# Expert products from two fp16 parts with power-of-two scales, and another order of loads, in an attention and mixture-of-experts kernel

## The chip, the cores and the metric

One core of one Trainium2 chip runs the whole program. The metric is the device time of one launch in microseconds (us), here the median of three runs. The profile is of one execution; its span runs from the first to the last instruction.

## The reference, cut to what matters

The input is x (16 batches of 100 tokens, 256 features). A cross-attention (16 heads, 361 context rows) adds to x. Then a soft mixture of experts adds again:

```python
x = x + xattn(layernorm(x), ctx, ctx, mask, ...)
z = layernorm(layernorm(x), norm_g, norm_b)
se = layernorm(slot_embeds, slot_g, slot_b) * scale
logits = einsum('bnd,esd->bnes', z, se)                  # 16 experts, 64 slots each
dispatch = softmax(logits, axis=tokens)
combine = softmax(logits over all 1024 slots)
slots = einsum('bnd,bnes->besd', z, dispatch)
gate = gelu(slots @ Wg[e] + bg[e])                       # 256 -> 512
up = slots @ Wu[e] + bu[e]
eout = (gate * up) @ Wd[e] + bd[e]                       # 512 -> 256
out = x + einsum('bns,bso->bno', combine, eout)
```

All inputs are fp32, and so is the output. The last row reads the x after attention.

## The kernel before, in words

The program has three blocks one after the other, with a barrier between them: `attention_phase`, `routing_phase` and `expert_phase`. Every engine has its own list of instructions, written out by hand; semaphores tie the lists together.

**Attention** treats the 16 batches in a pipeline. Its last steps also make the normalised tokens of batch 0 for routing (lines 577 to 599).

**Routing** treats one batch in each step t. PE makes the logits (L1167), ACT copies them to `l_sb` (L1075), DVE takes the maxima (L1002, L1024), ACT makes the exponentials (L1084, L1103), PE transposes, DVE and ACT copy to `dispT` and `combT`, and SP stores both to DRAM. DVE also makes the normalised tokens of a later batch (L1027 to L1048), which ACT keeps in `xn`. Between these steps the first two experts are made ready: `load_gate_up` (POOL), `weights_hi` (ACT) and `weights_lo` (DVE); and the last two steps make the first slots (`first_slots`, L1224, L1232, L1240).

**Experts.** The 16 experts come in 8 pairs: pair 0, a loop over pairs 1 to 6, pair 7. Each pair is treated for two halves h of the batches (8 batches, 512 rows of slots), each half for its two experts e, so there are 32 units u of work. In a unit, PE makes for each of four blocks c of 128 hidden features the `gate` and the `up` product (L1539). A product in fp32 is replaced by three products of two parts, a high and a low one:

```python
for wt, st in ((wgu_h, slot_h), (wgu_h, slot_l), (wgu_l, slot_h)):
    for kc in range(2):
        mm = nc.tensor.matmul(bank[:], wt[e][...], st[h][...], start=(k == 0), stop=(k == 5))
```

The high part is a copy rounded to float32r, the low part is the value minus the high one, also float32r. After the product of block c, ACT makes the gelu (`gate_sb`, L1486), DVE adds the bias of up and multiplies (L1430), ACT rounds to `hid_h` (L1490), DVE subtracts to `hid_l` (L1435). Behind block c PE also makes a piece of the slots of the next half (c = 0 and 2, L1512) or of the output of the last one (c = 1 and 3, L1519), both in plain fp32, with the pieces `slot_h` and `slot_l` (L1473, L1406) and the addition to x (L1415) behind them. Then come the 48 `down` products of the unit (L1579): in `DOWN_ORDER` the first 18 need `hid_h` and `hid_l` of blocks 0 to 2 only, the 19th needs block 3. DVE adds the bias `bd` and writes `eo` in two parts g (L1453); part 0 can start behind the 36th product. SP moves `eo` to `eo_pair`.

The weights of the next pair are split once per pair: `wgu_h` (L1274, ACT) and `wgu_l` (L1279, DVE) behind units (h=1, e=0) and (h=1, e=1), for expert 0 and 1; `wd_h` (L1496) and `wd_l` (L1441) inside the units of h=0, at c=1 and c=2. POOL issues the loads of weights, of `disp` and of `comb`, and waits for each buffer to come free.

## Time and profile before

| | us |
|---|---|
| median of 3 runs (1162.72 to 1166.11) | 1164.14 |
| the profiled execution | 1163.88 |
| its span | 1162.2 |
| PE busy | 1063.1 |
| DVE busy | 698.5 |
| ACT busy | 576.3 |
| POOL busy | 332.6 |

In the timeline attention ends at 356 us, routing at 501 us, and the experts take the rest. "Busy" of PE counts each matmul from its start to its modelled end; matmuls overlap, so their pace is read from start to start. The granted clock is given as a share of full speed: 1.00 is 2.4 GHz and 0.50 is 1.2 GHz.

### The profile page before, as it was taken

The numbers are of one execution on the slowest core, as the hardware profiler recorded it, in microseconds if no ns is written. First come the engines' busy times: TensorE is split into PE (matmuls) and PEld (weight loads), VectorE is DVE, ScalarE is ACT, GpSimd is POOL, SyncE is SP. The second block draws the span as 40 slices with busy tenths as digits, with TensorE's granted clock in tenths as the row PEclk, the third lists the DMA queues.
The fourth block names the chain that finished last, engine by engine and source line by source line (L and its number), as shares of the span: only waits on it lengthen the run. The fifth ranks groups of instructions, "written<-read, shape, count | busy, mean of one in ns | idle before, by whom it ended". The sixth has DMA issues, their size and how long they took to land.

```text
span 1162.2 us, 22171 instructions
## 1 busy us (share of the span) xinstructions
PE 1063.1 (91%) x7172; PEld 869.9 (75%) x7172; DVE 698.5 (60%) x1247; ACT 576.3 (50%) x1084; POOL 332.6 (29%) x348
## 2 busy tenths in 40 slices
PE   5688999999877888789999999999999999999997
PEld 3466777777663444478888888888888888888885
DVE  5556777777636888544555555655645555556544
ACT  2376878778655788733433343433424334333421
POOL 5267767667664343210010010100100100100000
PEclk8789999999958999889999999999999999999998
DMA  8858778678403534432142242432331331422123
GB/s 208 183 120 142 168 156 159 155 140 172 88 2 96 145 99 112 122 129 65 41 132 75 56 117 74 107 103 76 113 92 41 113 93 41 131 74 54 47 57 83
DMA packets 115080, 121.50 MB, mean 105 GB/s; under 512 B 46633, under 2 KB 105445, under 8 KB 115029
## 3 DMA queue, kind: packets, MB, share of 16 engines
q1 hardware_dynamic: 100908, 79.07, 30.5%
q0 software_dynamic: 10960, 40.67, 11.5%
q10 hardware_dynamic: 3160, 1.11, 0.6%
q8 instruction: 28, 0.46, 0.2%
q14 instruction: 24, 0.19, 0.1%
HBM read 73.87 MB, written 29.93 MB: 89 GB/s over the span
## 4 chain that ended last, share of the span: by engine, by line
PE 55%; DVE 1%; issue 1%; ACT 0%; DVEq 0%; ACTq 0%
PE down L1579 16%; PE gate L1539 15%; PE up L1539 15%; PE mix L1519 5%; PE mix L1512 4%; DVE gate_sb L1430 0%; ACT hid_h L1490 0%; DVE hid_l L1435 0%; DVE wd_l L1441 0%; DVE x L1415 0%; ACT gate_sb L1486 0%; DVE slot_l L1406 0%; DVEq L1633 0%; DVEq L1429 0%; DVEq L1412 0%
## 5 line engine op out<-in xcount | busy, mean ns | idle before, releaser
L1486 ACT ACTIVATE gate_sb<-gate,bgu 128x512 f32<-128x512 f32 x128 | 88.1, 689 | 222.3 <-PE gate L1539 207.7
L402 POOL TENSOR_TENSOR p_l<-p_f,p_h 121x800 f16<-121x800 f32 (+1 forms) x96 | 163.7, 1718 | 80.4 <-ACT p_h L652 79.5
L1490 ACT ACTIVATE hid_h<-gate_sb 128x512 fp32r<-128x512 f32 x128 | 80.9, 632 | 178.0 <-DVE gate_sb L1430 178.0
L1430 DVE SCALAR_TENSOR_TENSOR gate_sb<-up,bgu,gate_sb 128x512 f32<-128x512 f32 x128 | 95.9, 749 | 103.1 <-PE up L1539 101.3
L486 DVE TENSOR_REDUCE head_max<-at_rows 100x2 f32<-100x722 f32 x124 | 112.9, 910 | 71.8 <-PE at_rows L730 69.8
L1579 PE MATMUL down<-wd_h,hid_h 128*128 128x256 f32 x512 | 150.7, 294 | 0.7 <-DVE hid_l L1435 0.7
L1435 DVE TENSOR_TENSOR hid_l<-gate_sb,hid_h 128x512 fp32r<-128x512 f32 x128 | 88.6, 692 | 93.6 <-ACT hid_h L1490 93.6
L1579 PE MATMUL down<-wd_l,hid_h 128*128 128x256 f32 x512 | 144.8, 283 | 0.0
L1579 PE MATMUL down<-wd_h,hid_l 128*128 128x256 f32 x512 | 144.8, 283 | 0.0
L1263 POOL DMA_DIRECT2D wd<-in_Wd x16 | 12.2, 766 | 320.8 <-DVE eo L1453 300.4
L1579 PEld LDWEIGHTS down<-wd_h,hid_h 128*128 128x128 f32 x512 | 98.0, 191 | 3.4 <-issue 1.0
L1453 DVE TENSOR_TENSOR eo<-down,bd 128x512 f32<-128x512 f32 x64 | 44.3, 692 | 93.3 <-PE down L1579 93.3
L1579 PEld LDWEIGHTS down<-wd_l,hid_h 128*128 128x128 f32 x512 | 98.2, 192 | 0.8
L1579 PEld LDWEIGHTS down<-wd_h,hid_l 128*128 128x128 f32 x512 | 98.1, 192 | 0.0
L647 ACT ACTIVATE p_f<-at_cols 121x800 f32<-121x800 f32 (+1 forms) x96 | 79.7, 830 | 30.4 <-PE at_cols L742 29.4
L1539 PE MATMUL gate<-slot_h,wgu_h 128*128 128x512 f32 x256 | 91.0, 436 | 4.0 <-PEq L1631 4.0
L730 PE MATMUL at_rows<-kt,qt 100*100 100x362 f32 x248 | 74.5, 383 | 12.2 <-DVE head_max L486 11.4
L652 ACT ACTIVATE p_h<-p_f 121x800 f16<-121x800 f32 (+1 forms) x96 | 83.6, 871 | 3.0
L1539 PE MATMUL gate<-slot_l,wgu_h 128*128 128x512 f32 x256 | 80.7, 397 | 0.0
L1539 PE MATMUL up<-slot_l,wgu_h 128*128 128x512 f32 x256 | 80.1, 394 | 0.0
L742 PE MATMUL at_cols<-qt,kt 104*121 104x200 f32 (+1 forms) x384 | 67.8, 303 | 13.4 <-DMA qt<-max_p 8.8
L1539 PE MATMUL up<-slot_h,wgu_h 128*128 128x512 f32 x256 | 80.0, 394 | 0.0
(165 smaller groups left out, 2279.1 us busy)
## 6 DMA issues: line engine op xcount, KB each, us to landing
eo_pair<-eo SPq DMA_DIRECT2D x128, 128.0 KB, 2.4
k_parts<-kq_n SPq DMA_DIRECT2D x16, 724.0 KB, 3.7
kt<-k_parts SPq DMA_DIRECT2D x32, 362.0 KB
wgu<-in_Wg POOLq DMA_DIRECT2D x16, 512.0 KB, 6.2
wgu<-in_Wu POOLq DMA_DIRECT2D x16, 512.0 KB, 6.9
wd<-in_Wd POOLq DMA_DIRECT2D x16, 512.0 KB, 5.2
combine<-combT SPq DMA_DIRECT2D x16, 400.0 KB, 4.0
dispatch<-dispT SPq DMA_DIRECT2D x16, 400.0 KB
```

What stands on the lines that cost most here:

```text
L402: nc.gpsimd.tensor_tensor(p_l[i][0:kn, :, 0:N], p_f[i][0:kn], p_h[i][0:kn, :, 0:N], ALU.subtract).then_inc(p_low, 1)
L486: nc.vector.tensor_reduce(head_max[:, :, r], bank[0:N, :, 0:S], AX.X, ALU.max).then_inc(max_ready, 1)
L647: nc.scalar.activation(p_f[u][0:kn].rearrange("k (g e) n -> k g (e n)", g=2), cols_ps[0:kn, :, 0:4 * N], ACT.Exp, scale=1.0 / SCALE_INV).t ...
L652: nc.scalar.activation(p_h[u][0:kn, :, 0:N], p_f[u][0:kn], ACT.Copy).then_inc(p_hi, 1)
L730: mm = nc.tensor.matmul(bank[0:N, c, 0:SW], q[0:ROWS_A, r, N * c:N * c + N], k[0:ROWS_A, r, :], start=True, stop=True)
L742: mm = nc.tensor.matmul(cols_ps[0:kn, e // 2, (e % 2) * 2 * N:(e % 2 + 1) * 2 * N], kt[t % NBUF][0:ROWS_B, r, j * KC:j * KC + kn], qt[t % ...
L1430: nc.vector.scalar_tensor_tensor(gate[c % 2][:], up_ps[c % 2][:], bu_col(bgu, pair, e, c), gate[c % 2][:], ALU.add, ALU.mult).then_inc(hid ...
L1435: nc.vector.tensor_tensor(hid_l[:, c, :], gate[c % 2][:], hid_h[:, c, :].bitcast(F32), ALU.subtract).then_inc(hidl_ready, 1)
L1486: nc.scalar.activation(gate[c % 2][:], gate_ps[c % 2][:], ACT.Gelu, bias=bg_col(bgu, pair, e, c)).then_inc(gelu_ready, 1)
L1490: nc.scalar.activation(hid_h[:, c, :], gate[c % 2][:], ACT.Copy).then_inc(hidh_ready, 1)
L1539: mm = nc.tensor.matmul(bank[:], wt[e][:, kc, i, c * P:(c + 1) * P], st[h][:, kc, e, :, :].rearrange("p b s -> p (b s)"), start=(k == 0), ...
L1579: mm = nc.tensor.matmul(down_ps[t // 2][:, t % 2, :], ht[:, c, t * P:(t + 1) * P], wt[:, c, :], start=(c == 0 and k == 0), stop=(c == FC - ...
```

## The change

**Types.** `wgu_h`, `wgu_l`, `wd_h`, `wd_l`, `slot_h`, `slot_l`, `hid_h` and `hid_l` become float16 in place of float32r. The list of matmuls on PE is the same, instruction by instruction. Accumulation stays in fp32.

**Scales.** A float16 has little range, so every operand is multiplied by a power of two. For the slots the scale comes from a bound, the largest magnitudes of `norm_g` and `norm_b` (new `norm_scaled` on DVE at the end of attention; both vectors are multiplied once, and the logits are divided again in the copy to `l_sb`). For the weights it comes from the largest magnitude of each expert's weights: new reductions on DVE (`max_gate_up`, `max_down`, `max_hidden_bias`), which give a maximum per partition; SP stores them to DRAM and reads all of them back to every partition (`share_maxima`); then `expert_scales` on DVE makes a chain of 14 small operations, with a wait between those that depend on each other. Copies to high parts get a `scale` operand on ACT, and the subtractions to low parts on DVE become SCALAR_TENSOR_TENSOR (multiply, subtract), as does the addition of `bd`. ACT gets a marker instruction (`sem_inc(waited)`) ahead of `hid_h` and `wd_h`.

**Order.** The maxima of the next pair are taken in unit (h=0, e=1) for gate and up and in (h=1, e=0) for down, the scales in (h=1, e=1) at c=2. Both `wgu_h` and both `wgu_l` now come behind unit (h=1, e=1). The loads of `Wd` and of half of `disp` come earlier in POOL's list, the load of `bd` apart from that of `Wd`. In routing `wgu_h` of expert 0 moves from t=1 to t=15, ahead of the copy to `l_sb`; `wgu_l` of expert 0 too moves to t=15; the maxima stand at t=1, 2 and 12, the scales at t=14.

**Semaphores.** Several are merged into one; nothing else in attention moves.

The core of the diff:

```diff
-        "wgu_h": [sb(f"wgu_h{e}", [P, 2, 2, F], F32R) for e in range(2)],
-        "wgu_l": [sb(f"wgu_l{e}", [P, 2, 2, F], F32R) for e in range(2)],
+        "wgu_h": [sb(f"wgu_h{e}", [P, 2, 2, F], F16) for e in range(2)],
+        "wgu_l": [sb(f"wgu_l{e}", [P, 2, 2, F], F16) for e in range(2)],
         "wd": [sb(f"wd{e}", [P, FC, D], F32) for e in range(2)],
...
         def step(b, t):
             for s in range(SLOTS_RT):
                 part(s + SLOTS_RT, b - 1, t - 1)
                 part(s, b, t)
-            if t == 1:
+            if t in (1, 2):
+                max_gate_up(nc, dve, keep, t - 1, 0)
+            if t == B - 4:
+                for e in range(2):
+                    max_down(nc, dve, keep, e, 0)
+                dve.wait_ge(keep["bias_in"], 32)
+                max_hidden_bias(nc, dve, keep, 0)
+            if t == B - 2:
+                expert_scales(nc, dve, keep, 0)
+            if t == B - 1:
                 weights_lo(nc, dve, keep, 0, 0)
             if t in (B - 1, B):
...
+def share_maxima(eng, keep, pair):
+
+    eng.wait_ge(keep["max_ready"], MAXIMA * pair + MAXIMA)
+    eng.sem_inc(keep["waited"], 1)
+    if not (isinstance(pair, int) and pair == 0):
+        eng.wait_ge(keep["scale_step"], SCALE_STEPS * pair)
+    eng.sem_inc(keep["waited"], 1)
+    flat = keep["max_dram"]
+    eng.dma_start(flat.rearrange("(p j) -> p j", p=P), keep["maxima"][:].rearrange("p k e -> p (k e)")).then_inc(keep["max_moved"], 16)
+    eng.wait_ge(keep["max_moved"], 32 * pair + 16)
+    eng.sem_inc(keep["waited"], 1)
+    eng.dma_start(keep["all_maxima"][:], flat.partition_broadcast(P)).then_inc(keep["max_moved"], 16)
+
...
+def expert_scales(nc, dve, keep, pair):
...
+    def done(n):
+        dve.wait_ge(step, SCALE_STEPS * pair + n)
+        dve.sem_inc(keep["waited"], 1)
+
+    dve.wait_ge(keep["max_moved"], 32 * pair + 32)
+    if not (isinstance(pair, int) and pair == 0):
+        done(0)
+    nc.vector.tensor_reduce(top[:, 0:3, :].rearrange("p k e -> p (k e)"), keep["all_maxima"][:].rearrange("q (p j) -> q j p", p=P), AX.X, ALU.max).then_inc(step, 1)
+    done(1)
...
 def weights_hi(nc, act, keep, e, pair):
     act.wait_ge(keep["wgu_in"][e], 32 * pair + 32)
-    nc.scalar.activation(keep["wgu_h"][e][:], keep["wgu"][e][:], ACT.Copy).then_inc(keep["wh_ready"][e], 1)
+    act.wait_ge(keep["scale_step"], SCALE_STEPS * pair + SCALE_STEPS)
+    act.sem_inc(keep["waited"], 1)
+    nc.scalar.activation(keep["wgu_h"][e][:], keep["wgu"][e][:], ACT.Copy, scale=keep["w_scale"][:, bass.ds(pair, 1), 0, e]).then_inc(keep["wh_ready"][e], 1)
 
 
 def weights_lo(nc, dve, keep, e, pair):
     dve.wait_ge(keep["wh_ready"][e], pair + 1)
-    nc.vector.tensor_tensor(keep["wgu_l"][e][:], keep["wgu"][e][:], keep["wgu_h"][e][:].bitcast(F32), ALU.subtract).then_inc(keep["wl_ready"][e], 1)
+    dve.sem_inc(keep["waited"], 1)
+    nc.vector.scalar_tensor_tensor(keep["wgu_l"][e][:], keep["wgu"][e][:], keep["w_scale"][:, bass.ds(pair, 1), 0, e], keep["wgu_h"][e][:],
+                                   ALU.mult, ALU.subtract).then_inc(keep["wl_ready"][e], 1)
 
...
                         for odd in range(2):
                             sp.dma_start(dst[:, 2 * g:2 * g + 2, odd, :], eo[e][odd * SL:(odd + 1) * SL, 2 * g:2 * g + 2]).then_inc(eo_moved[h][e][g], 16)
+                    if h == 1 and e == 0 and not last:
+                        share_maxima(sp, keep, pair + 1)
...
-                pool.wait_ge(slots_done, 4 * (2 * pair + 2))
+                pool.wait_ge(wdl_ready[0], pair + 1)
                 pool.sem_inc(waited, 1)
-                for h in range(2):
-                    hb = slice(BH * h, BH * h + BH)
-                    pool.dma_start(disp[:, hb], at(dispatch_dram, pair + 1)[:, hb]).then_inc(disp_in[h], 16)
+                load_down(pool, a, keep, 0, pair + 1)
+                load_slot_weights(pair + 1, 0, 4 * (2 * pair + 1))
             if not first:
                 pool.wait_ge(comb_done, 8 * pair)
                 pool.sem_inc(waited, 1)
                 pool.dma_start(comb[:], at(combine_dram, pair)).then_inc(comb_in, 16)
             if not last:
+                pool.wait_ge(wdl_ready[1], pair + 1)
+                pool.sem_inc(waited, 1)
+                load_down(pool, a, keep, 1, pair + 1)
+                load_slot_weights(pair + 1, 1, 4 * (2 * pair + 2))
                 for e in range(2):
                     pool.wait_ge(eo_ready, 2 * (4 * pair + 2 + e) + 2)
                     pool.sem_inc(waited, 1)
-                    load_down(pool, a, keep, e, pair + 1)
+                    load_down_bias(pool, a, keep, e, pair + 1)
...
                         if not (first and h == 0 and e == 0):
                             dve.wait_ge(down_done, 2 * u)
-                        nc.vector.tensor_tensor(hid_l[:, c, :], gate[c % 2][:], hid_h[:, c, :].bitcast(F32), ALU.subtract).then_inc(hidl_ready, 1)
+                        nc.vector.scalar_tensor_tensor(hid_l[:, c, :], gate[c % 2][:], keep["hid_scale"][:, bass.ds(2 * pair + e, 1)], hid_h[:, c, :],
+                                                       ALU.mult, ALU.subtract).then_inc(hidl_ready, 1)
                         if h == 0 and c == 2:
 
                             dve.wait_ge(wdh_ready[e], pair + 1)
                             if not first:
                                 dve.wait_ge(down_done, 2 * u - 2)
-                            nc.vector.tensor_tensor(wd_l[e][:], wd[e][:], wd_h[e][:].bitcast(F32), ALU.subtract).then_inc(wdl_ready[e], 1)
+                            nc.vector.scalar_tensor_tensor(wd_l[e][:], wd[e][:], keep["w_scale"][:, bass.ds(pair, 1), 1, e], wd_h[e][:],
+                                                           ALU.mult, ALU.subtract).then_inc(wdl_ready[e], 1)
                         r = 2 * e + c // 2
                         if c % 2 == 0 and nxt:
                             dve.wait_ge(slots_done, 4 * (hs + 1) + r + 1)
                             slots_lo(hs + 1, 1 - h, r)
                         if c % 2 == 1 and prev:
                             combine_add(hs - 1, 1 - h, r, first)
+                        if h == 1 and e == 1 and c == 2 and not last:
+                            expert_scales(nc, dve, keep, pair + 1)
                     for g in range(2):
+                        if h == 0 and e == 1 and not last:
+                            max_gate_up(nc, dve, keep, g, pair + 1)
+                        if h == 1 and e == 0 and not last:
+                            max_down(nc, dve, keep, g, pair + 1)
+                            if g == 1:
+                                max_hidden_bias(nc, dve, keep, pair + 1)
                         dve.wait_ge(down_done, 2 * u + g + 1)
                         if not (first and h == 0):
                             dve.wait_ge(eo_moved[1 - h][e][g], 32 * pair + 32 * h)
-                        dve.wait_ge(wd_in[e], 32 * pair + 32)
-                        nc.vector.tensor_tensor(eo[e][:, 2 * g:2 * g + 2, :], down_ps[g][:],
-                                                bd[e][:].rearrange("p (o d) -> p o d", o=1).broadcast_to([P, 2, D]), ALU.add).then_inc(eo_ready, 1)
-                    if h == 1 and not last:
-                        weights_lo(nc, dve, keep, e, pair + 1)
+                        dve.wait_ge(keep["bd_in"][e], 16 * pair + 16)
+                        dve.sem_inc(waited, 1)
+                        nc.vector.scalar_tensor_tensor(eo[e][:, 2 * g:2 * g + 2, :], down_ps[g][:], keep["un_down"][:, bass.ds(2 * pair + e, 1)],
+                                                       bd[e][:].rearrange("p (o d) -> p o d", o=1).broadcast_to([P, 2, D]),
+                                                       ALU.mult, ALU.add).then_inc(eo_ready, 1)
+                        if h == 1 and e == 1 and not last:
+                            weights_lo(nc, dve, keep, g, pair + 1)
             if last:
                 for r in range(4):
                     combine_add(2 * pair + 1, 1, r, False)
...
-                        weights_hi(nc, act, keep, e, pair + 1)
+                    if h == 1 and e == 1 and not last:
+                        for x in range(2):
+                            act.wait_ge(up_done, FC * (u - 1 + x) + FC)
+                            weights_hi(nc, act, keep, x, pair + 1)
 
         pairs(act, step)
```

**The order of instructions** is shown at two places. The first is DVE in the loop over the pairs, unit (h=1, e=1), from c=3 to the jump back. Before (`gate_sb` is the product of gate and up, `eo` the expert's output, `wgu_l` the low part of the next pair's weights):

```order
L1430 SCALAR_TENSOR_TENSOR gate_sb<-up,bgu,gate_sb 128x512
L1435 TENSOR_TENSOR hid_l<-gate_sb,hid_h 128x512
L1410 REGISTER_ALU
L1415 SCALAR_TENSOR_TENSOR x<-mix,rz,x 100x256 x2
L1449 REGISTER_ALU
L1453 TENSOR_TENSOR eo<-down,bd 128x512
L1449 REGISTER_ALU
L1453 TENSOR_TENSOR eo<-down,bd 128x512
L1279 TENSOR_TENSOR wgu_l<-wgu,wgu_h 128x2048
L1331 REGISTER_ALU
L1331 COMPARE_AND_BRANCH
```

Now, in the changed kernel:

```order
L1581 SCALAR_TENSOR_TENSOR gate_sb<-up,bu_s,gate_sb 128x512
L1586 SCALAR_TENSOR_TENSOR hid_l<-gate_sb,hid_scale,hid_h 128x512
L1561 REGISTER_ALU
L1566 SCALAR_TENSOR_TENSOR x<-mix,rz,x 100x256 x2
L1610 REGISTER_ALU
L1615 SCALAR_TENSOR_TENSOR eo<-down,un_down,bd 128x512
L1415 REGISTER_ALU
L1417 SCALAR_TENSOR_TENSOR wgu_l<-wgu,w_scale,wgu_h 128x2048
L1610 REGISTER_ALU
L1615 SCALAR_TENSOR_TENSOR eo<-down,un_down,bd 128x512
L1417 SCALAR_TENSOR_TENSOR wgu_l<-wgu,w_scale,wgu_h 128x2048
L1470 REGISTER_ALU
```

`wgu_l` of expert 0 has come in between the two `eo`. Ahead of this piece, behind `slot_l` of c=2, stand the 14 operations on `top`, `w_scale`, `un_gate`, `bu_s`, `hid_scale` and `un_down`, which were not there before.

The second place is ACT in routing at t=15. Before, the piece was:

```order
L1084 ACTIVATE e_comb,z_tok<-l_sb,neg_max 100x1024
L1103 ACTIVATE e_disp,z_slot<-rt_lT,neg_max_s 128x100 x8
L1075 ACTIVATE l_sb<-rt_logits 100x1024
L1274 ACTIVATE wgu_h<-wgu 128x2048
L1091 ACTIVATE combT<-rt_out 128x400 x2
L1232 ACTIVATE slot_h<-rt_slots 128x4x2x64
L1232 ACTIVATE slot_h<-rt_logits 128x4x2x64
```

and now:

```order
L1147 ACTIVATE e_disp,z_slot<-rt_lT,neg_max_s 128x100 x8
L1411 ACTIVATE wgu_h<-wgu,w_scale 128x2048
L1118 ACTIVATE l_sb<-rt_logits,norm_top 100x1024
L1411 ACTIVATE wgu_h<-wgu,w_scale 128x2048
L1135 ACTIVATE combT<-rt_out 128x400 x2
L1281 ACTIVATE slot_h<-rt_slots 128x4x2x64
L1281 ACTIVATE slot_h<-rt_logits 128x4x2x64
```

The copy to `l_sb` of the last batch stands behind `wgu_h` of expert 0, and that one waits for the scales.

## Rows read from the trace of the kernel before

**Rows 1.** The page, part 1: busy time of each engine, share, instructions.
```profile
PE 1063.1 (91%) x7172; PEld 869.9 (75%) x7172; DVE 698.5 (60%) x1247; ACT 576.3 (50%) x1084; POOL 332.6 (29%) x348
```

**Rows 2.** Windows of 40 us: PE, PEld, DVE, ACT, POOL busy (instructions), clock, DMA share, GB/s.
```profile
840.00:880.00 40.00, 40.00 (x239) 35.19 (x238) 21.42 (x34) 13.13 (x21) 1.68 (x3) 1.00 0.26 72
880.00:920.00 40.00, 40.00 (x239) 35.25 (x238) 23.98 (x34) 16.28 (x23) 5.44 (x8) 1.00 0.36 95
```

**Rows 3.** The page, part 5: ACT's first parts, busy, mean ns, idle before.
```profile
L1490 ACT ACTIVATE hid_h<-gate_sb 128x512 fp32r<-128x512 f32 x128 | 80.9, 632 | 178.0 <-DVE gate_sb L1430 178.0
```

**Rows 4.** Timeline of PE in a pair: start, length in us, engine, line, instruction.
```profile
807.62 0.62 PE L1539 MATMUL gate<-slot_l,wgu_h 128*128 128x512 f32 x2
...
809.44 0.62 PE L1539 MATMUL up<-slot_h,wgu_l 128*128 128x512 f32 x2
...
821.53 0.47 PE L1579 MATMUL down<-wd_h,hid_h 128*128 128x256 f32 x1
821.84 0.28 PE L1579 MATMUL down<-wd_l,hid_h 128*128 128x256 f32 x1
...
827.35 0.28 PE L1579 MATMUL down<-wd_h,hid_l 128*128 128x256 f32 x1
```

**Rows 5.** Timeline of PE in attention: first and last of 15 16-bit matmuls in a row.
```profile
204.49 0.18 PE L762 MATMUL at_out<-v,p_l 121*128 121x49 bf16 x1
...
204.84 0.18 PE L762 MATMUL at_out<-v,p_l 121*128 121x49 bf16 x1
```

**Rows 6.** Timeline of DVE in routing: small operations one behind the other.
```profile
418.91 1.22 DVE L1002 TENSOR_REDUCE neg_max<-l_sb 100x1 f32<-100x1024 f32 x1
420.05 0.15 DVE L1007 RECIPROCAL rz<-z_tok 100x1 f32 x1
420.12 0.56 DVE L1024 TENSOR_REDUCE neg_max_s<-rt_lT 128x4 f32<-128x400 f32 x1
...
422.03 0.18 DVE L1038 BATCH_NORM_AGGREGATE rt_mv<-rt_st 100x2 f32<-100x6 f32 x1 [0.15 <-DVE rt_st L1035]
```

**Rows 7.** Timeline of DVE, h=1, e=1, from c=2 to the first eo.
```profile
817.40 0.75 DVE L1430 SCALAR_TENSOR_TENSOR gate_sb<-up,bgu,gate_sb 128x512 f32<-128x512 f32 x1 [0.71 <-PE up L1539]
...
819.46 0.68 DVE L1406 TENSOR_TENSOR slot_l<-mix,slot_h 128x512 fp32r<-128x512 f32 x1
821.05 0.75 DVE L1430 SCALAR_TENSOR_TENSOR gate_sb<-up,bgu,gate_sb 128x512 f32<-128x512 f32 x1 [0.92 <-PE up L1539]
822.50 0.69 DVE L1435 TENSOR_TENSOR hid_l<-gate_sb,hid_h 128x512 fp32r<-128x512 f32 x1 [0.70 <-ACT hid_h L1490]
...
826.23 0.69 DVE L1453 TENSOR_TENSOR eo<-down,bd 128x512 f32<-128x512 f32 x1 [2.25 <-PE down L1579]
```

**Rows 8.** Timeline of DVE: end of attention; routing at t=1 and t=14.
```profile
338.58 0.56 DVE L518 TENSOR_REDUCE o_sum<-at_out 100x128 f32<-100x384 f32 x1 [5.15 <-PE at_out L762]
...
377.02 2.29 DVE L1279 TENSOR_TENSOR wgu_l<-wgu,wgu_h 128x2048 fp32r<-128x2048 f32 x1 [0.46 <-ACT wgu_h L1274]
...
481.61 1.29 DVE L1018 COPY dispT<-rt_out 100x512 f32<-100x512 f32 x2 [3.31 <-PE rt_out L1152]
```

**Rows 9.** Timeline of ACT: the last batch of routing.
```profile
481.37 1.07 ACT L1075 ACTIVATE l_sb<-rt_logits 100x1024 f32<-100x1024 f32 x1
482.27 1.97 ACT L1274 ACTIVATE wgu_h<-wgu 128x2048 fp32r<-128x2048 f32 x1
```

**Rows 10.** Timeline of DVE, h=0, e=0: gate of c=2 and hid_l of c=3.
```profile
837.84 0.75 DVE L1430 SCALAR_TENSOR_TENSOR gate_sb<-up,bgu,gate_sb 128x512 f32<-128x512 f32 x1 [0.71 <-PE up L1539]
...
843.08 0.69 DVE L1435 TENSOR_TENSOR hid_l<-gate_sb,hid_h 128x512 fp32r<-128x512 f32 x1 [0.70 <-ACT hid_h L1490]
```

**Rows 11.** Timeline of PE: start of the down products of that half.
```profile
841.86 0.47 PE L1579 MATMUL down<-wd_h,hid_h 128*128 128x256 f32 x1
```

**Rows 12.** Timeline of PE in routing: the same products at the two clocks.
```profile
468.21 6.12 PE L1167 MATMUL rt_logits<-seT,rt_xnT 128*100 128x512 f32 x8 [2.94 <-ACT rt_xnT L1112]
...
477.46 3.68 PE L1167 MATMUL rt_logits<-seT,rt_xnT 128*100 128x512 f32 x8
```

206 lines of the change are left out of this document (149 added, 57 removed).

## Prediction

> **What bounds the kernel now.** I read the views in this order. The page's busy times show PE in front, 1063.1 of 1162.2 us, with DVE at 698.5 [rows 1]. That is a mean over three blocks, so the windows come next: in the expert block PE is busy for 40.00 of every 40 us at a clock of 1.00 (2.4 GHz), while DVE has 21.4 and 24.0 and ACT 13 and 16 [rows 2]. Two thirds of the time are thus PE's own pace, and the wait of ACT's `hid_h` for DVE, 178.0 us in sum, costs nothing [rows 3]. The timeline gives that pace. Eight gate and up products lie between 807.62 and 809.44: 0.2275 us each for 512 columns. The down products start every (827.35 − 821.84)/46 = 0.1198 us for 256 columns [rows 4]. At 2.4 GHz the columns alone would take 0.2133 and 0.1067, so a float32r product pays a surcharge of 14.2 and 13.1 ns. Last I read how late DVE delivers what PE needs, because the change gives DVE more work at three places.
>
> I count in the time of the profiled execution, 1163.88 us (span 1162.2, so 1.7 lie around it); the median is 0.3 above it. About 0.3% can be told from no change, 3.5 us.
>
> **PE's products.** Their list stays. The nearest row for a 16-bit pair of weight load and product is attention's: 14 steps from 204.49 to 204.84, 25.0 ns for 49 columns, of which 20.4 are columns; surcharge 4.6 ns [rows 5]. So short a product may be held by something else, so I take 3.5 ns; the bounds are 0 (bare columns) and 14 (no gain). Gate and up gain 10.7 ns, down 9.6. A unit has 48 of each: 0.51 + 0.46 = 0.97 us; 32 units: **−31** (bounds −42 and 0). The Trainium skill, TensorE: Matmul & The Clock Gate, section Back-to-back issue gap, gives columns over 2.4 plus 2.5 ns for a warm product; by it the gain would be −34.
>
> **Scales at the end of each pair (7 times).** `expert_scales` stands on DVE behind `slot_l` of c=2 in unit (h=1, e=1), ahead of the multiplication of c=3, behind which `hid_h`, `hid_l` and PE's 19th down product are queued. No row shows this chain; I build it. A reduction of 1024 took 1.22 and one of 400 took 0.56, which makes 0.93 for its 768 elements. A small operation takes 0.15, an independent one starts 0.07 behind the last, and a dependent one 0.15 behind the end of its source [rows 6]. Eight waits: 0.93 + 8×0.15 + the operations, 7×0.15 + 6×0.08 = 3.7 us. The bounds: all back to back, 0.93 + 13×0.07 = 1.8; twice the handover, since in the loop each wait needs register work, 5.
>
> Where it bites, counted from the multiplication of c=2 at 817.40 [rows 7]: `slot_l` ends 2.74 later. The marker on ACT and the change of `hid_l` from TENSOR_TENSOR (0.69) to SCALAR_TENSOR_TENSOR (0.75) add 0.06 + about 0.1 (estimate: the difference between a handover with a marker, 0.15 [rows 6], and one without, half of 0.70 − 0.63 [rows 3, 7]). The chain starts at 2.9 and ends at 6.6. From the multiplication of c=3 to the end of `hid_l` it is 822.50 + 0.69 − 821.05 = 2.14, with 0.16 added 2.3: 8.9, and PE hears it at 9.0. PE wants it for its 19th product: 821.84 + 17×0.12 − 817.40 = 6.5 before, and 0.3 less with quicker products: 6.2. **Stall 2.8 us.**
>
> The data for the chain are there: the maxima end with unit (1,0), two DMAs of 2 to 3 us follow, and the chain stands some 17 us behind. The maxima themselves (two of 2.3 us in (0,1), two of 1.2 in (1,0)) lie beside PE's down products: DVE is idle for 2.25 us ahead of the first `eo` [rows 7], and they end before the next unit's first multiplication, so I cost them at nothing. With that cover gone they would cost up to 2 us a pair. All the added work, some 12 us a pair, raises DVE from 23 to 29 of 40 us: not a bound.
>
> **`wgu_l` of expert 0 (7 times).** Before, it lay behind unit (1,0), with a whole unit to spare. Now it lies between the two `eo` of (1,1), and PE's next instruction is a gate product that waits for it. The first `eo` starts at 826.23; the down products end at 827.35 + 0.12 = 827.47, 1.24 later [rows 4, 7], with quicker products 1.12. DVE needs 0.75 for `eo` (SCALAR_TENSOR_TENSOR now) and 2.29 + 0.06 for `wgu_l` [rows 8]: ready 2.0 behind the end, with the handover **2.1 us** of stall. The bounds are 1.8 and 2.4. ACT has both `wgu_h` done by then (2×1.97 [rows 9] from the end of `hid_h` of c=3). `wgu_l` of expert 1 ends about when the first multiplication of the new pair is due. Both stalls: 4.9 × 7 = **+34** (bounds 7×2.7 = 19 and 7×6.4 = 45).
>
> **Units of h=0.** From the multiplication of c=2 (837.84) to the end of `hid_l` of c=3 (843.77) it is 5.93 [rows 10]; here `wd_l` stands in between and DVE is full, so every addition counts: two markers and three changes to SCALAR_TENSOR_TENSOR, 0.4. With the handover 6.5. PE wants it at 841.86 + 0.31 + 17×0.12 − 837.84 = 6.4 [rows 4, 11], now 6.1. Stall 0.4, 15 units: **+6** (0 to 8). In units of h=1 0.2 us are left over, so no stall.
>
> **Routing.** At t=1 a reduction of 2048 takes the place of `wgu_l` (2.29 [rows 8]), and ACT loses a copy; the one at t=2 is new on the busiest engine: together +1.5 (0 to 2.5). At t=12 the added 2.6 us meet the stretch in which the logits ran at half the clock (6.12 us against 3.68 [rows 12]) and all waited for them: +0.2. At t=14 the scales start when `dispT` ends (482.8 [rows 8]), 3.7, handover 0.2, `wgu_h` 1.9, and only then `l_sb`, which started at 481.37 [rows 9]: it starts at 488.6, 7.2 late, and everything to the block's end hangs on it. `wgu_l` at t=15 delays the last `rz_slot` by 1 more. Sum **+10** (5 to 13).
>
> **Attention.** `norm_scaled` (3 us) falls into DVE's idle 5.15 us ahead of 338.58 [rows 8]: 0. The moved loads of `Wd` and `disp` only come earlier, and `comb` now goes ahead of half of `disp`: 0. SP waits in `share_maxima` while it has nothing else: 0.
>
> **Sum:** 1163.9 − 31 + 34 + 6 + 10 = 1183 us. The gain is real, but the price of getting the scales is larger.
>
> **Rivals.**
> 1. *VectorE gets quicker too.* If its operations with 16-bit operands ran at twice the pace, `wgu_l` would take 1.3 in place of 2.3, and `hid_l` and `slot_l` 0.3 less each. Second stall −1.0, first −0.9, h=0 gone, routing −1.5: 1183 − 7×1.9 − 6 − 1.5 = 1162; with the chain at its lower bound (−1.9 at 8 places) **1147**. It ends on the faster side once the low parts save 1 us at a boundary and the chain is under 3.3. For it: types are halved. Against: one operand of each is still fp32. Chance 0.08.
> 2. *The 16-bit product beats its columns.* The same section of the skill also gives about 131 ns per product for a stream of 512-column pairs. As a mechanism of this kernel: PE would fall behind DVE, which has 29 of 40 us of work and waits for ACT in each block; a unit would take some 16 us in place of 20.3, and the time about 1040. The 25 ns for 49 columns [rows 5] speak against it. Chance 0.02.
> 3. *The clock falls at the boundaries.* PE stands still for 2.8 and 2.1 us with 3.3 us of work between. In routing, an idle 2.94 us ended in logits at half the clock (1.2 GHz) [rows 12]. Each boundary would then run a few us at half pace and lose about 2.5: 1183 + 18 = **1201**. Against it: the engine is full before and behind. Chance 0.15.
> 4. *The change doesn't do what it says:* the surcharge belongs to any load of 128 columns. Then 1183 + 31 = **1214**. The 16-bit rows of attention [rows 5] speak against it. Chance 0.04.
> 5. *The chain is short,* 2 us or less, as its operations overlap, and the surcharge is gone entirely: 1183 − 8×1.8 − 11 = **1158**. For it: the 0.07 between independent operations. Against: eight links are dependent. Chance 0.1.
>
> My forecast, 1170 to 1195 with its own bounds, has 0.61. The range of 8 in 10 goes from 1157 to 1201: it leaves out rivals 2 and 4 and half of 1. Faster by over 0.3%: rivals 1 (0.07), 2 and 5 (0.06): 0.15. Within 0.3%: the rest of rival 5 and the low end of mine, 0.06. Slower: 0.79.
>
> **What would show it.** Gate spacing 0.217 and down spacing 0.110; PE idle ahead of the 19th down product of (1,1) by 2.8 us, released by `hid_l`; idle ahead of the first gate product of a pair by 2.1, released by `wgu_l`; idle of 0.4 in the down products of h=0; the expert block starting near 511 in place of 501.4. I am wrong if the spacing stays at 0.228 and 0.120, if PE shows no idle time at the boundary, or if the chain on `top` takes under 2 us or over 5.

## The result, and the profile after

| | before | after |
|---|---|---|
| median, us | 1164.39 (4 runs) | 1215.23 (4 runs, 1212.36 to 1217.61) |
| the profiled execution, us | 1163.88 | 1217.13 |
| its span, us | 1162.2 | 1215.5 |

The ratio of after to before is 1.0435, with a 95% interval of 1.0404 to 1.0467: 51 us slower. The forecast had the sign (slower, chance 0.79) and the places, but said 19 us slower with a range up to 1201. The time lies outside it.

The page of the changed kernel, part 1, and windows of its expert block (columns as in [rows 1, 2]):

```profile
PE 1058.3 (87%) x7172; PEld 707.6 (58%) x7172; DVE 794.4 (65%) x1409; ACT 602.4 (50%) x1084; POOL 333.3 (27%) x349
...
800.00:840.00 40.00, 39.63 (x246) 25.46 (x245) 28.32 (x39) 14.83 (x21) 1.89 (x3) 1.00 0.24 70
840.00:880.00 40.00, 33.58 (x178) 19.80 (x176) 24.34 (x42) 17.14 (x21) 3.96 (x6) 0.91 0.32 95
```

PE is no longer busy for 40 of 40 us. A window without the end of a pair still has 39.6 at full clock; one with it has 33.6, and the granted clock is under 1. So most of the loss in the expert block sits at the ends of pairs. PE's timeline at one of them (unit (h=1, e=1) and the first products of the next pair) shows what:

```profile
767.18 0.27 PE L1747 MATMUL down<-wd_h,hid_l 128*128 128x256 f16 x1
...
768.49 0.27 PE L1747 MATMUL down<-wd_h,hid_l 128*128 128x256 f16 x1
773.13 0.27 PE L1747 MATMUL down<-wd_h,hid_h 128*128 128x256 f16 x1 [4.37 <-DVE hid_l L1586]
...
774.49 0.42 PE L1747 MATMUL down<-wd_h,hid_l 128*128 128x256 f16 x1
774.70 0.42 PE L1747 MATMUL down<-wd_h,hid_h 128*128 128x256 f16 x1
...
777.96 0.27 PE L1747 MATMUL down<-wd_h,hid_l 128*128 128x256 f16 x1
779.66 0.59 PE L1707 MATMUL gate<-slot_h,wgu_h 128*128 128x512 f16 x2 [1.43 <-DVE wgu_l L1417]
...
782.24 1.06 PE L1680 MATMUL mix<-disp,xn 100*128 100x128 f32 x8
```

The spacings first: 12 down products from 767.18 to 768.49, 0.1092 us each (0.1198 before, [rows 4]); 12 gate and up products from 779.66 to 782.24, 0.215 us (0.2275 before). Then an idle time of 4.37 us ahead of the 19th down product, released by `hid_l`. Then a stretch in which the same products start 0.21 apart; the granted clock is 0.50 there (1.2 GHz). Between 774.1 and 777.6 some sixteen products lose 0.1 us each, 1.7 us. Then an idle time of 1.43 us for `wgu_l`. At the next pair end that one was 2.05, and the slow stretch came in two pieces, the second behind the stall for `wgu_l`:

```profile
866.22 0.96 PE L1707 MATMUL gate<-slot_h,wgu_h 128*128 128x512 f16 x2 [2.05 <-DVE wgu_l L1417]
866.97 1.06 PE L1707 MATMUL gate<-slot_l,wgu_h 128*128 128x512 f16 x2
...
870.06 0.59 PE L1707 MATMUL up<-slot_h,wgu_l 128*128 128x512 f16 x2
```

DVE's timeline ahead of the 773.13 of PE, from the multiplication of c=2 to `hid_l` of c=3:

```profile
762.39 0.75 DVE L1581 SCALAR_TENSOR_TENSOR gate_sb<-up,bu_s,gate_sb 128x512 f32<-128x512 f32 x1 [0.26 <-PE up L1707]
...
765.31 1.51 DVE L1378 TENSOR_REDUCE top<-all_maxima 128x6 f32<-128x768 f32 x1
766.99 0.17 DVE L1381 TENSOR_SCALAR top<-top 128x4 f32<-128x4 f32 x1 [0.16 <-DVE top L1378]
...
768.78 0.59 DVE L1393 TENSOR_SCALAR bu_s<-bgu,w_scale,norm_top  x2 [0.28 <-DVE top L1390]
...
770.38 0.16 DVE L1404 SCALAR_TENSOR_TENSOR un_down<-top 128x2 f32 x1
770.58 0.75 DVE L1581 SCALAR_TENSOR_TENSOR gate_sb<-up,bu_s,gate_sb 128x512 f32<-128x512 f32 x1
772.23 0.75 DVE L1586 SCALAR_TENSOR_TENSOR hid_l<-gate_sb,hid_scale,hid_h 128x512 f16<-128x512 f32 x1 [0.90 <-ACT hid_h L1655]
```

The chain starts 2.92 us behind the multiplication (forecast 2.9) and takes 5.3 to the next one, 765.31 to 770.58 (forecast 3.7, upper bound 5).

From the starts of the units in PE's timeline, a table of the six pairs of the loop (four units each, start to start, us):

| kernel | (0,0) | (0,1) | (1,0) | (1,1) | mean pair |
|---|---|---|---|---|---|
| before | 20.32 | 20.32 | 20.32 | 20.32 | 81.3 |
| after | 19.86 to 21.56 | 19.85 | 19.2 to 19.4 | 27.0 to 27.8 | 87.0 |

At least two of four units, and mostly three, are faster than before. The fourth gives back more than all four gain. The first unit has 21.56 where a slow stretch runs into it. The granted clock falls to 0.50 behind the stalls at all seven pair ends.

Routing: the expert block's first gate product starts at 516.60 (501.37 before). ACT's timeline of the last batch, which answers to [rows 9], and the `dispT` of that batch on DVE:

```profile
485.69 0.26 ACT L1147 ACTIVATION_READ_ACCUMULATOR e_disp<-rt_lT,neg_max_s 128x1 f32 x1
492.20 2.00 ACT L1411 ACTIVATE wgu_h<-wgu,w_scale 128x2048 f16<-128x2048 f32 x1 [6.25 <-DVE un_down L1404]
494.11 1.10 ACT L1118 ACTIVATE l_sb<-rt_logits,norm_top 100x1024 f32<-100x1024 f32 x1
...
486.02 1.29 DVE L1050 COPY dispT<-rt_out 100x512 f32<-100x512 f32 x2 [3.31 <-PE rt_out L1194]
```

`l_sb` starts 8.1 us behind the `dispT` of that batch (486.02); before, it started 0.2 ahead of it (481.37 and 481.61, [rows 8, 9]).

The start of the expert block also holds what attention took in that one execution: the first `l_sb` of routing came at 363.43 here, at 362.50 before, and between 361 and 369 in the profiles of the experiments, which leave attention as it is. So routing is best counted from its first `l_sb` to the first gate product: 138.9 us before, 153.2 after, 14.3 more.

### The profile page after: what moved, and what is told of

The parts are those of the page before. It is cut to its first block, busy times and chain, and to the rows that moved or that the text cites. A ratio compares the mean times of both kernels' runs of the same rounds, so it can differ in the third digit from the quotient of the medians.

```text
span 1215.5 us, 22832 instructions
## 1 busy us (share of the span) xinstructions
PE 1058.3 (87%) x7172; PEld 707.6 (58%) x7172; DVE 794.4 (65%) x1409; ACT 602.4 (50%) x1084; POOL 333.3 (27%) x349
## 3 DMA queue, kind: packets, MB, share of 16 engines
q10 hardware_dynamic: 3160, 1.11, 0.5%
## 4 chain that ended last, share of the span: by engine, by line
PE 43%; DVE 7%; issue 4%; ACT 2%; DMA 0%; DVEq 0%; ACTq 0%
PE gate L1707 13%; PE up L1707 12%; PE down L1747 11%; PE mix L1680 4%; PE mix L1687 3%; DVE gate_sb L1581 2%; ACT hid_h L1655 2%; DVE hid_l L1586 2%; DVE wgu_l L1417 1%; DVE top L1378 1%; DMA disp<-dispatch 0%; ACT slot_h L1636 0%; DVE slot_l L1557 0%; DVE wd_l L1593 0%; ACT wd_h L1663 0%
## 5 line engine op out<-in xcount | busy, mean ns | idle before, releaser
L1649 ACT ACTIVATE gate_sb<-gate,bgu,un_gate 128x512 f32<-128x512 f32 x128 | 99.2, 775 | 207.6 <-PE gate L1707 201.5
L1655 ACT ACTIVATE hid_h<-gate_sb,hid_scale 128x512 f16<-128x512 f32 x128 | 92.4, 722 | 207.2 <-DVE gate_sb L1581 207.2
L1747 PE MATMUL down<-wd_h,hid_h 128*128 128x256 f16 x512 | 146.0, 285 | 38.9 <-DVE hid_l L1586 36.8
L1586 DVE SCALAR_TENSOR_TENSOR hid_l<-gate_sb,hid_scale,hid_h 128x512 f16<-128x512 f32 x128 | 96.2, 752 | 121.5 <-ACT hid_h L1655 121.5
L1747 PE MATMUL down<-wd_l,hid_h 128*128 128x256 f16 x512 | 146.0, 285 | 0.0
L1747 PE MATMUL down<-wd_h,hid_l 128*128 128x256 f16 x512 | 146.0, 285 | 0.0
L1581 DVE SCALAR_TENSOR_TENSOR gate_sb<-up,bu_s,gate_sb 128x512 f32<-128x512 f32 x128 | 96.0, 750 | 59.8 <-PE up L1707 52.4
L1707 PE MATMUL gate<-slot_h,wgu_h 128*128 128x512 f16 x256 | 77.3, 384 | 15.6 <-DVE wgu_l L1417 10.4
L1707 PE MATMUL up<-slot_h,wgu_h 128*128 128x512 f16 x256 | 77.5, 385 | 0.0
L1707 PE MATMUL gate<-slot_h,wgu_l 128*128 128x512 f16 x256 | 77.5, 385 | 0.0
L1707 PE MATMUL gate<-slot_l,wgu_h 128*128 128x512 f16 x256 | 77.4, 384 | 0.0
```

The lines of the kernel that those rows point to most:

```text
L1581: nc.vector.scalar_tensor_tensor(gate[c % 2][:], up_ps[c % 2][:], keep["bu_s"][:, bass.ds(2 * pair + e, 1), c], gate[c % 2][:], ALU.add, A ...
L1586: nc.vector.scalar_tensor_tensor(hid_l[:, c, :], gate[c % 2][:], keep["hid_scale"][:, bass.ds(2 * pair + e, 1)], hid_h[:, c, :], ALU.mult, ...
L1649: nc.scalar.activation(gate[c % 2][:], gate_ps[c % 2][:], ACT.Gelu, bias=bg_col(bgu, pair, e, c), scale=keep["un_gate"][:, bass.ds(2 * pai ...
L1655: nc.scalar.activation(hid_h[:, c, :], gate[c % 2][:], ACT.Copy, scale=keep["hid_scale"][:, bass.ds(2 * pair + e, 1)]).then_inc(hidh_ready, 1)
L1707: mm = nc.tensor.matmul(bank[:], wt[e][:, kc, i, c * P:(c + 1) * P], st[h][:, kc, e, :, :].rearrange("p b s -> p (b s)"), start=(k == 0), ...
L1747: mm = nc.tensor.matmul(down_ps[t // 2][:, t % 2, :], ht[:, c, t * P:(t + 1) * P], wt[:, c, :], start=(c == 0 and k == 0), stop=(c == FC - ...
```

## The experiments

Four kernels separate the parts, one separates the clock from the wait that it follows, and five try the places of the added work. All times are medians, beside runs of the kernel before on the same chip (medians of 1163.9 to 1166.1). The changed kernel itself was not run again beside them; differences from it are taken from the median above, 1215.23, and its runs spread over 5 us.

### 1. The types alone

```diff
-        "wgu_h": [sb(f"wgu_h{e}", [P, 2, 2, F], F32R) for e in range(2)],
+        "wgu_h": [sb(f"wgu_h{e}", [P, 2, 2, F], F16) for e in range(2)],
...
-    ... keep["wgu_h"][e][:].bitcast(F32), ALU.subtract)
+    ... keep["wgu_h"][e][:], ALU.subtract)
```

(in the kernel before, and the same for the other seven operands)

> The kernel before with float16 in place of float32r and nothing else (no scales, no maxima, the old order); the products' parts are rounded to float16 without a scale, so low parts lose bits. My theory: a product costs 0.2155 us (512 columns) and 0.1093 us (256) as in the changed kernel, 1.08 us less in each of 32 units, and no boundary has a stall, so the clock stays at 1.00 in the expert block: 1164 - 34.6 = 1130 us (1126 to 1134). Rival A (the clock falls because 16-bit products run faster or harder, not because of the stall): stretches of half clock are seen in the expert block of this kernel too, about 2.3 us per pair, 1146 us. Rival B (DVE becomes the bound at h=0 with quicker products): stalls of 0.2 to 0.4 us ahead of the 19th down product in h=0, 1134 to 1137.

Measured: 1126.85 us (1125.90 to 1128.49); ratio 0.9679 [0.9652, 0.9705]. A steady pair took 76.60 us, with PE busy in all of it and the clock at 1.00:

```profile
600.00:640.00 40.00, 40.00 (x254) 26.53 (x253) 23.76 (x35) 15.38 (x23) 2.98 (x5) 1.00 0.29 74
```

So the products give 81.29 − 76.60 = 4.69 us in each of the six pairs of the loop, and with 3.5 in pair 0 and 4.6 in the last pair the expert block is 36.3 us shorter. The other 1.7 of the profile lie ahead of that block. Half-clock stretches do not belong to 16-bit products (rival A falls). The table of DVE and ACT by form from 620 to 1100 us in this kernel, beside the changed one, tells what the 16-bit types and the scales do to the other engines. Kernel f16_plain:

```profile
L1435 DVE TENSOR_TENSOR hid_l<-gate_sb,hid_h 128x512 f16<-128x512 f32 x101 | 69.9, 692 | 74.1 <-ACT hid_h L1490 74.1
L1490 ACT ACTIVATE hid_h<-gate_sb 128x512 f16<-128x512 f32 x102 | 64.2, 629 | 137.2 <-DVE gate_sb L1430 137.2
L1279 DVE TENSOR_TENSOR wgu_l<-wgu,wgu_h 128x2048 f16<-128x2048 f32 x12 | 27.4, 2281 | 0.0
```

The changed kernel:

```profile
L1586 DVE SCALAR_TENSOR_TENSOR hid_l<-gate_sb,hid_scale,hid_h 128x512 f16<-128x512 f32 x89 | 66.9, 751 | 86.1 <-ACT hid_h L1655 86.1
L1655 ACT ACTIVATE hid_h<-gate_sb,hid_scale 128x512 f16<-128x512 f32 x89 | 64.2, 722 | 146.9 <-DVE gate_sb L1581 146.9
L1417 DVE SCALAR_TENSOR_TENSOR wgu_l<-wgu,w_scale,wgu_h 128x2048 f16<-128x2048 f32 x10 | 23.4, 2342 | 0.0
```

DVE makes a 16-bit `hid_l` in 692 ns, as it made the float32r one [rows 7]: it gains nothing from the type. And ACT pays about 90 ns for a scale that comes from memory (629 to 722).

### 2. The scales alone

```diff
-        "wgu_h": [sb(f"wgu_h{e}", [P, 2, 2, F], F16) for e in range(2)],
+        "wgu_h": [sb(f"wgu_h{e}", [P, 2, 2, F], F32R) for e in range(2)],
```

(in the changed kernel, and the same for the other seven operands)

> The changed kernel with float32r in place of float16 (scales, maxima, order of loads as changed; the 3 KB of all maxima share the space of combT from pair 1 on). My theory: the products are 1.08 us per unit slower (+34.6), the stall of the chain is 4.1 in place of 4.4 as PE arrives 0.3 later, the small stall in h=0 is 0.1 in place of 0.38, and the clock still falls behind the stall: 1215 + 34.6 - 2 - 4 = 1244 us (1238 to 1250). Rival A (the half clock belongs to 16-bit products): no half-clock stretch, about 1228. Routing as in the changed kernel, the first gate product near 516.

Measured: 1243.19 us (1238.50 to 1244.81); ratio 1.0659 [1.0623, 1.0696]. The scales, the maxima and their order cost 77 us by themselves. The stall ahead of the 19th down product was 4.11 us at the steady pair ends, and half-clock stretches that lost 1.6 to 3.7 us followed there, with float32r operands throughout. `hid_h` took 724 ns on ACT, so the 90 ns belong to the scale, not to the output type. The types gain 39 us in the old order (experiment 1) but only 28 in the new one (1243 − 1215): in the new one PE reaches the waits sooner and stands there longer (4.37 in place of 4.11 us ahead of the 19th down product), which takes part of the gain back.

### 3. Without the chain

```diff
-                        if h == 1 and e == 1 and c == 2 and not last:
-                            expert_scales(nc, dve, keep, pair + 1)
```

(all pairs read the scales of pair 0)

> The changed kernel without the chain of scales for pairs 1 to 7: all experts use the scales of the first pair (left out: the scales from the other pairs' own maxima; the maxima are still taken and shared). My theory: the stall of 4.37 us ahead of the 19th down product goes at 7 boundaries (30.6), and with it the half-clock stretches behind it (2.3 us per pair in sum, 16); the stall for wgu_l at the next pair stays at 1.4 to 2.0. 1215 - 46 = 1169 us (1165 to 1175). Rival A (half clock not due to the stall): 1215 - 31 = 1184. Rival C (chain is not what delays hid_l, it is the extra DVE work in general): the stall shrinks by less than half, over 1195.

Measured: 1180.81 us (1177.40 to 1186.23); ratio 1.0127 [1.0096, 1.0159]. 34 us less, not 46. The stall ahead of the 19th down product is gone. But the one for `wgu_l` was 2.15 us at each pair end, and behind it the clock still fell:

```profile
766.46 0.59 PE L1705 MATMUL gate<-slot_h,wgu_h 128*128 128x512 f16 x2 [2.15 <-DVE wgu_l L1417]
...
768.13 1.06 PE L1705 MATMUL up<-slot_h,wgu_h 128*128 128x512 f16 x2
768.99 1.06 PE L1705 MATMUL up<-slot_l,wgu_h 128*128 128x512 f16 x2
...
771.63 0.60 PE L1705 MATMUL gate<-slot_h,wgu_h 128*128 128x512 f16 x2
```

This was so at all seven pair ends, and unit (0,0) took 21.5 us in place of 19.86. My expectation charged the first stall with the whole of the clock; one stall of 2.15 us was enough for it here.

### 4. Products in place of the idle time

```diff
+                        if t == 0 and cs[0] == FC - 1 and h == 1 and e == 1 and not last:
+                            pe.wait_ge(gelu_ready, FC * u + 3)
+                            for _ in range(36):
+                                nc.tensor.matmul(gate_ps[0][:, 0:D], hid_h[:, 0, 0:P], wd_h[e][:, 0, :], start=True, stop=True)
...
+                    if h == 0 and e == 0 and not first:
+                        for _ in range(12):
+                            nc.tensor.matmul(gate_ps[0][:, 0:D], ...
```

> The changed kernel with products into a free PSUM bank where PE stands still: 36 of 256 columns (3.9 us) ahead of the 19th down product of unit (h=1, e=1), 12 (1.3 us) ahead of the first gate product of a pair. They compute nothing that is used; the waits for hid_l and wgu_l stay as late as they were. Theory (the clock falls because PE stood still): no half-clock stretch at the boundaries, 2.3 us less per pair, 1215 - 16 = 1199 us (1194 to 1206). Rival (the clock falls for another reason: DVE's or ACT's work, or 16-bit products at full pace): the half-clock stretches stay, 1215 (1212 to 1220).

Measured: 1200.99 us (1198.54 to 1208.32); ratio 1.0303 [1.0270, 1.0335]. The wait for `hid_l` ends as late as it did, 20.47 us behind the start of unit (1,1) in both kernels. The one for `wgu_l` ends 5.59 us behind it in place of 6.53, since the down products ahead of `eo` now run at full clock. The kernel is 14 us faster than the changed one, and the clock stays up:

```profile
771.75 1.47 PE L1748 MATMUL gate<-wd_h,hid_h 128*128 128x256 f16 x12
773.66 0.27 PE L1754 MATMUL down<-wd_h,hid_h 128*128 128x256 f16 x1 [0.44 <-DVE hid_l L1586]
...
776.93 1.47 PE L1700 MATMUL gate<-slot_h 128*128 128x256 f16 x12
779.25 0.59 PE L1710 MATMUL gate<-slot_h,wgu_h 128*128 128x512 f16 x2 [0.85 <-DVE wgu_l L1417]
```

Two windows with a pair end each (columns as above) have a granted clock of 1.00, where the changed kernel had 0.91:

```profile
760.00:800.00 40.00, 38.33 (x259) 26.10 (x258) 26.86 (x46) 15.88 (x19) 4.71 (x7) 1.00 0.34 102
840.00:880.00 40.00, 38.72 (x249) 25.67 (x248) 26.74 (x45) 18.52 (x23) 5.29 (x8) 1.00 0.32 93
```

A steady pair took 85.0 us (864.25 − 779.25) in place of 87.0. The price of the clock alone is 2.0 us per pair, 14 in all, and idle PE is its cause: filled with work that nothing uses, it does not arise.

### 5. The chain in two parts

```diff
                         if h == 1 and e == 1 and c == 2 and not last:
                             expert_scales(nc, dve, keep, pair + 1)
+                        if h == 1 and e == 1 and c == 3 and not last:
+                            hidden_scales(nc, dve, keep, pair + 1)
```

(`hidden_scales` is the part from `bu_s` on)

> The changed kernel with the chain cut in two: the part up to w_scale, un_gate and the bound (3.0 us) stays behind slot_l of c=2, the rest (2.3 us) moves behind c=3's addition to x, into DVE's idle time ahead of the first eo. My theory: the stall ahead of the 19th down product is 2.1 in place of 4.4, the one for wgu_l grows from 1.6 to about 3 as the first eo and wgu_l of expert 0 come later. Whether a stall of 2.1 still brings the clock down decides: if it does, 1215 - 7*0.8 = 1209; if it takes the clock fall with it, 1215 - 7*2.8 = 1195. Rival C (the sum of DVE's work counts, not where the chain stands): 1215, no change.

Measured: 1192.93 us (1190.07 to 1195.95); ratio 1.0250 [1.0219, 1.0281]. The stall shrank to 2.3 us, the one for `wgu_l` was 1.8 to 2.2 (not 3), and unit (1,1) took 23.9 to 25.6 us in place of 27: behind the shorter stall the clock fell at four of the seven pair ends. That makes the 1193 lower than the 1195 stated for no fall at all, because routing gave some us too: `wgu_h` waits for the first part alone, and the last `l_sb` came 6.4 us behind its `dispT` in place of 8.1 (the first gate product came at 513.3, of which another 1.8 lie in attention). Rival C falls: DVE did the same work, and the kernel took 22 us less.

### 6. The layout of the reduction

```diff
-    ... keep["all_maxima"][:].rearrange("q (p j) -> q j p", p=P), AX.X, ALU.max)
+    ... keep["all_maxima"][:].rearrange("q (j p) -> q j p", p=P), AX.X, ALU.max)
```

> The changed kernel with the reduction over all maxima reading 128 elements side by side in place of every sixth (the kinds of maxima are mixed by that, the rest is the same). Theory 1 (the every-sixth reading made the reduction 1.51 us in place of the 0.93 that the row of 1024 elements gave): the reduction takes 0.95, the chain 4.7, the first stall 3.8. Theory 2 (a reduction into six results costs more by itself): 1.5 us stays, and the time stays at 1215.

Measured: 1204.18 us (2 runs, 1202.80 and 1205.56); ratio 1.0346 [1.0319, 1.0373]. The operations on `top` in this kernel (min/median/max in ns):

```profile
L1378 DVE TENSOR_REDUCE top<-all_maxima x8: 941/942/944, 485.5 to 1102.2; 128x6 f32<-128x768 f32 x8
```

The same view of the changed kernel:

```profile
L1378 DVE TENSOR_REDUCE top<-all_maxima x8: 1479/1510/1518, 487.2 to 1112.1; 128x6 f32<-128x768 f32 x8
```

0.942 us is close to the 0.93 that the prediction worked out from contiguous rows (a straight line through its two rows gives 0.95, [rows 6]); reading every sixth element added 0.57. The Trainium skill (SBUF — State Buffer, the note on cachelines in Door 1) says that reads which step past a 16-byte line at each element pay a penalty; six fp32 elements are 24 bytes, and the trace agrees. The stall fell to 3.79. That is 0.57 × 8 = 5 us of the 11 gained, the eighth of them in routing. The rest I can only place, not prove. At two of the seven pair ends the clock stayed at 1.00 here, and no slow stretch ran into unit (0,0) at any. One of the two:

```profile
767.67 0.27 PE L1747 MATMUL down<-wd_h,hid_h 128*128 128x256 f16 x1 [3.79 <-DVE hid_l L1586]
...
773.26 0.59 PE L1707 MATMUL gate<-slot_h,wgu_h 128*128 128x512 f16 x2 [2.16 <-DVE wgu_l L1417]
```

The same two stalls, 3.79 and 2.16, left the clock up here, while in experiment 3 one of 2.15 brought it down at every pair end. So the length of the idle time alone does not tell whether the clock falls.

### 7. A later wait for `wgu_l`

```diff
-                    pe.wait_ge(wl_ready[e], pair + 1)
+                    pe.wait_ge(keep["wh_ready"][e], pair + 1)
...
+                                if wt is wgu_l and c == 0 and i == 0:
+                                    pe.wait_ge(wl_ready[e], pair + 1)
```

> The changed kernel with PE's wait for wgu_l moved from the head of a unit to the first product that reads it, the 5th gate product of c=0 (the head waits for wgu_h). Theory: four products (0.86 us) run ahead of the wait, so the stall for wgu_l shrinks from 1.4 to 2.1 to about 0.6 to 1.2, the first stall stays: 1215 - 7*0.86 = 1209; if the shorter stall also shortens the half-clock stretches, down to 1203. Rival (wgu_h is as late as wgu_l): no change, 1215.

Measured: 1209.30 us (1204.69 to 1210.92); ratio 1.0370 [1.0332, 1.0409]. The stall fell to between 0.2 and 1.1 us. A new one of 0.4 us appeared in (0,0) ahead of the slots' piece of c=2, which waits for `x`: DVE stayed as late as it was. The clock still fell at each pair end. So about 6 of the 51 us hang on this wait; the runs of the two kernels do not overlap (1212.4 is the lowest of the changed one), but the intervals of their ratios touch.

### 8. Routing

```diff
-            if t in (1, 2):
-                max_gate_up(nc, dve, keep, t - 1, 0)
+            if t == 1:
+                max_gate_up(nc, dve, keep, 0, 0)
             if t == B - 4:
+                max_gate_up(nc, dve, keep, 1, 0)
...
+                if t == B - 2 and s == AT_RT["dispT_out"][0]:
+                    expert_scales(nc, dve, keep, 0)
...
-                if t == B - 1:
-                    weights_hi(nc, act, keep, 0, 0)
                 nc.scalar.activation(l_sb[:], ...
```

> The changed kernel with its additions to routing placed in idle time: maxima of expert 1 from t=2 to t=12, the scales in two parts ahead of dispT at t=14 and t=15, wgu_h of expert 0 behind the copy to l_sb, that of expert 1 to t=16, wgu_l of expert 0 behind slot_l at t=15, that of expert 1 to the head of the expert block. The expert block's own chain is unchanged. Theory (8.3 us come from the wait of l_sb for wgu_h and the scales, 3 from the maxima at t=2, 2.5 from wgu_l): the first gate product near 504 in place of 516.6, 1215 - 12 = 1203 us (1199 to 1208). Rival (the work on DVE and ACT counts wherever it stands): first gate product at 513 or later, 1211 or more.

Measured: 1201.55 us (1196.41 to 1206.28); ratio 1.0312 [1.0264, 1.0361]. The first gate product started at 504.08. Counted from the first `l_sb`, routing took 142.9 us, 10.3 less than in the changed kernel; the profiles of experiments 9 and 10, which place this work in the same way, have 138.0 and 139.0, against 138.9 before the change. So the 14.3 us that routing lost were a matter of place: most or all of them go with the same work done in idle time.

### 9. and 10. Everything in idle time

```diff
-                        if h == 1 and e == 1 and c == 2 and not last:
-                            expert_scales(nc, dve, keep, pair + 1)
...
+                        if h == 1 and e == 0 and g == 0 and not last:
+                            expert_scales(nc, dve, keep, pair + 1)
+                        if h == 1 and e == 1 and g == 0 and not last:
+                            weights_lo(nc, dve, keep, 0, pair + 1)
```

(two of the moves; the expectation names the others)

> The routing of routing_early, and in the expert block: maxima of down at c=0 and c=1 of unit (h=1, e=0), shared ahead of the eo stores; the first part of the chain in DVE's idle time ahead of the first eo of (1,0), the second at c=0 of (1,1); wgu_h of expert 0 on ACT at c=1 of (1,1), its wgu_l ahead of the first eo of (1,1); wgu_h and wgu_l of expert 1 as before at the end. All scales are computed as in the changed kernel. Theory (only the places of the added work cost, not its sum, 29 of 40 us on DVE): no stall over 0.5 us and no half clock at the pair boundaries, 0.4 us in each h=0 unit stay; expert block 624.5 + 16*0.4 = 631 from 505: 1138 us (1130 to 1148). Rival (DVE's added work shows wherever it is put): stalls of about 1 us or more in the units that take it, 1160 or more.

Measured: 1159.28 us (1154.41 to 1167.89, 7 runs); ratio 0.9953 [0.9919, 0.9988]. The stalls at the pair ends were gone and with them every half-clock stretch there. But the time was not 1138; it was next to the rival's 1160, and stalls of over 1 us had appeared, as the rival said. What made them decides between the two. DVE's timeline of unit (1,1), at c=0 and c=1:

```profile
815.12 0.47 DVE L1408 TENSOR_SCALAR bu_s<-bgu,w_scale,norm_top  x2
...
816.73 0.16 DVE L1419 SCALAR_TENSOR_TENSOR un_down<-top 128x2 f32 x1
816.92 0.75 DVE L1597 SCALAR_TENSOR_TENSOR gate_sb<-up,bu_s,gate_sb 128x512 f32<-128x512 f32 x1
...
819.24 0.87 DVE L1582 SCALAR_TENSOR_TENSOR x<-mix,rz,x 100x256 f32<-100x256 f32 x2
```

PE's piece of slots at c=2 waits for exactly that addition to x: PE stood idle for 1.23 us there and for 0.72 in (1,0), where the maxima stood in the same way. So the second version takes the work out from between `slot_l` and `x`:

```diff
-                        if h == 1 and e == 1 and c == 0 and not last:
+                        if h == 1 and e == 1 and c == 1 and not last:
                             hidden_scales(nc, dve, keep, pair + 1)
```

(against experiment 9; the maxima move too)

> scaled_best with DVE's extra work taken away from between slot_l and the addition to x, on which PE's next piece of slots waits (0.72 us in unit (1,0), 1.23 in (1,1) per pair there): maxima of gate and up ahead of the first eo of (0,0) and of (0,1), those of down ahead of the second eo of (0,1) and behind x at c=1 of (1,0), the second part of the chain behind x at c=1 of (1,1). Theory (the place decides): both stalls go, with their 0.16 each of restart 2.3 us per pair: 1159 - 16 = 1143 us (1139 to 1149). Rival (DVE's sum of work moves the same stall elsewhere): 1155 or more.

Measured: 1147.60 us (1145.07 to 1148.29); ratio 0.9853 [0.9832, 0.9874]. It computes all scales as the changed kernel does and is 1.5% faster than the kernel before. The theory's range held (1139 to 1149), and its rival (1155 or more) falls. Its windows:

```profile
760.00:800.00 40.00, 39.59 (x250) 25.72 (x248) 28.67 (x40) 14.75 (x21) 1.88 (x3) 1.00 0.34 97
800.00:840.00 40.00, 39.12 (x244) 25.24 (x242) 29.36 (x50) 18.32 (x23) 5.28 (x8) 1.00 0.36 101
```

DVE has 28.7 and 29.4 of 40 us, more per window than in the changed kernel, and the clock is at 1.00: the amount of its work did not make the stalls at the pair ends. It is not free either: a pair takes 79.1 us, and most of the 2.5 over 76.6 are three stalls of about 0.4 ahead of 19th down products, each with the 0.16 that a stall counts beyond its idle time (worked out below).

## Why the prediction was wrong

The places of the losses were right. The step that failed is the clock: the sum put it at nothing, and it cost 14 to 19 us. The second is the size of the chain on DVE, taken at 3.7 us where it took 5.3, and with it the stalls. Smaller terms were off too:

| term | forecast | measured | from |
|---|---|---|---|
| PE's products | −31 | −36 | experiment 1, the expert block |
| stalls at 7 pair ends | +34 | +44 | 7 × (4.53 + about 1.8) |
| the clock behind them | 0 | +19 | what is left of a pair, 7 × (10.4 − 4.53 − 1.8 − 1.3) |
| units of h=0 | +6 | +10 | 15 × 0.66 |
| routing | +10 | +14 | 153.2 − 138.9 |

Together they make 51 to 52, and 51 was measured (53 in the profiled execution, with 0.9 of it in attention). The 10.4 is 87.0 − 76.6, and 1.3 are the two units of h=0. A stall counts 0.16 more than its idle time, since that starts at the modelled end of a product: from 768.49 to 773.13 it is 4.64 less one spacing of 0.11, 4.53.

How the 63 us of the pair ends divide between stalls and clock depends on what one takes away first. With the clock held up (experiment 4) the waits cost 7 × (85.0 − 76.6 − 1.3) = 50, and the clock 14. There the wait for `wgu_l` is longer, for PE reaches it sooner.

Two things in the sum were luck: the gain of PE's products was taken 5 too small, which brought 1183 nearer to the result than its prices deserved, and the h=0 term below.

**PE's products.** The step "I take 3.5 ns" of surcharge was too careful: the spacing of 0.215 is 1.7 ns over the columns (0.2133), of 0.1092 some 2.5 ns. The Trainium skill (TensorE: Matmul & The Clock Gate, Back-to-back issue gap) gives 2.5 ns over the columns for a product at full clock; the trace agrees at 256 columns and has 0.8 less at 512. By the spacings 48 × 0.0125 + 48 × 0.0106 = 1.11 us per unit, 35.5; 36.3 was measured. The small rest is a balance at the seams between groups: the first down product took 0.31 before ([rows 4]) and 0.11 now, while the pieces of slots and output that PE makes behind the blocks became 0.54 longer per unit in sum.

**The chain.** "0.93 + 8×0.15 + the operations" gave 3.7; it took 5.3. Three things were missed: the reduction reads every sixth element (+0.57, experiment 6); four operations with a factor read from memory took 0.22 to 0.29 each, where 0.08 to 0.15 stood in the sum; and a few handovers took 0.25 to 0.28 in the loop. The bound for it was given as "twice the handover", 5, and even that was under the value, because the bound left the reduction at its contiguous price. Stall forecast 2.8, measured 4.37 of idle time, 4.53 in all.

I also wrote that the chain stands some 17 us behind its data. That was wrong: the chain starts 11.6 us behind the maxima, which end at 753.75; the second DMA is issued at 759.39 and takes 3.4 us to land (the median of its row), so at 762.8, 2.5 us ahead of the chain at 765.31. It cost nothing here, but it closes the way to an earlier place unless the maxima move too, as in experiments 9 and 10.

**The clock.** This is the step that failed most. Rival 3 had it, with "[rows 12]" as its evidence and a price of 2.5 us per pair end that is close to the 2.0 of experiment 4. But it had a chance of 0.15, because "the engine is full before and behind", and the sum had nothing for it. Idle times of 3.8 to 4.5 and 1.1 to 2.2 us brought the clock down at all seven pair ends, and in experiment 3 one of 2.15 alone did. With the clock held up the same kernel took 1201 us (experiment 4), the top of the stated range: the stalls alone lead to its edge, and the clock beyond it. A stall and the clock behind it had to be one case, not two.

**`wgu_l`.** Forecast 2.1 of stall; measured 1.1 to 2.2 in the changed kernel and 2.15 in experiment 3, where the clock is full in the down products. Where these run at half clock PE arrives later and the stall is shorter: the two costs partly cover each other.

**h=0.** The idle time was as forecast, 0.4 (0.37 to 0.39):

```profile
789.59 0.75 DVE L1581 SCALAR_TENSOR_TENSOR gate_sb<-up,bu_s,gate_sb 128x512 f32<-128x512 f32 x1 [0.35 <-ACT gate_sb L1649]
...
795.35 0.75 DVE L1586 SCALAR_TENSOR_TENSOR hid_l<-gate_sb,hid_scale,hid_h 128x512 f16<-128x512 f32 x1 [0.90 <-ACT hid_h L1655]
...
796.25 0.27 PE L1747 MATMUL down<-wd_h,hid_h 128*128 128x256 f16 x1 [0.39 <-DVE hid_l L1586]
```

From the multiplication of c=2 (789.59) to the end of `hid_l` (795.35 + 0.75) it was 6.51, against 5.93 in [rows 10] and 6.5 in the forecast. That it fits is partly luck, since the part of ACT was left out of the sum: 90 ns for each `gate_sb` and `hid_h`. The Trainium skill (ScalarE: Activation LUTs, What ACT_TABLE_LOAD costs) says that each per-partition pointer operand of an ACTIVATE adds about 93 ns; 629 to 722 in experiment 1 agrees. A unit lost 0.66 (19.85 − 19.19): the idle time and its 0.16 make 0.54, and 0.1 was lost by the units of h=1 without a stall too (19.21 and 19.12).

**Routing.** The slip of `l_sb` against `dispT` was forecast at 7.2 and measured at 8.3: the chain again. The first `l_sb` came 0.9 later than before, that of batch 14 4.4 later (478.77 and 474.37): 3.5 for the maxima at t=1, 2 and 12, where 1.7 was taken. The 0.9 is not `norm_scaled`: DVE was 1.6 late already ahead of it (325.96 in place of 324.36) and 1.1 behind it, so that cost nothing, as forecast. The last 2.5 lie behind `l_sb`, where 1 was taken for `wgu_l` at t=15. These three make the 14.3.

**Rivals 1, 2, 4 and 5** fell: DVE did 16-bit output at the old pace (692 ns), no 512-column product of the experts ran under its columns (0.215 us), the surcharge went with float32r (0.2275 to 0.215), and the chain was long (5.3).

What stays open: at which pair ends the clock falls was not settled. Behind stalls of about 2.3 and 2.2 us it fell at some and not at others (experiment 5), and behind 3.79 and 2.16 too (experiment 6).

## What to carry to other kernels

A wait on the engine that sets the pace can cost more than its length: here 2.0 us of half clock behind some 6 us of idle PE, so a stall and the clock behind it belong in one estimate. Before adding work to an engine that is 60% busy, ask what is queued behind it at that point: the same added work cost 88 us at its first places (1215 − 1127) and 21 at others (1148 − 1127), and that decided the sign. When a price is built from rows of like operations, compare their access pattern and their operands too (every sixth element: 1.51 in place of 0.94; a scale from memory on ACT: 722 in place of 629 ns).

## What was not expected of the hardware

- An ACTIVATE of 128x512 took 629 to 632 ns without and 722 to 724 ns with a scale read per partition, for 16-bit and for float32r output alike.
- TENSOR_REDUCE over 768 elements took 942 ns side by side and 1510 ns with every sixth element.
- Products whose result nothing reads, put into PE's idle time, kept the clock at 1.00 through all pair ends and made the kernel 14 us faster, with the wait for `hid_l` as late as before.
- A single idle time of 2.15 us, with PE busy around it, was followed by a granted clock of 0.50 at all seven pair ends of experiment 3; 3.79 and 2.16 us were not at two of the seven of experiment 6.
- DVE's TENSOR_TENSOR with one 16-bit input and 16-bit output took 692 ns for 512 elements, the time of the float32r form.
